# Sixteen tiles of expert-row sums: all on VectorE, or ten on VectorE and six on GpSimd

## What is computed

```
# layer 0: 16 experts, 2 for each token; layer 1: 32 experts, 8 for each token
for e in range(N_EXPERTS):
    h = silu(flat @ Wu[e]) * (flat @ Wg[e])
    out = out + combine[:, e:e + 1] * (h @ Wd[e])
...
routed = (down[unsort].reshape(T, K, H) * tkw[..., None]).sum(axis=1)
...
x = x + ffn(layernorm(x))
```

## Time and profile before

| | us |
|---|---|
| median of 3 runs | 1419.74 |
| lowest and highest | 1417.56 and 1423.05 |
| the profiled execution | 1433.71 |
| its span, first to last instruction | 1431.9 |
| layer 0, first load of yk to end of the last sum | 557.44 to 579.02 |
| layer 1, first load of yk to end of the last sum | 1371.67 to 1427.90 |

### The profile page before, as it was taken

How to read it: one execution, slowest core, us unless ns; L and a number is a source line. 1 busy time by engine, 2 the same in 40 slices (tenths; PEclk the granted TensorE clock), 3 DMA queues, 4 the chain that set the end, 5 groups by cost and what they waited for, 6 DMA issues and landing times. The chain is left out here.

```text
span 1431.9 us, 22633 instructions
## 1 busy us (share of the span) xinstructions
PE 1010.7 (71%) x6358; PEld 827.7 (58%) x6358; DVE 740.1 (52%) x1996; ACT 426.4 (30%) x1045; POOL 541.5 (38%) x740
## 2 busy tenths in 40 slices
PE   0289999998687894489998878660003999999910
PEld 0177777777554683377777756430003888887810
DVE  1677877774452355666555625620001555554567
ACT  1144444443110341134444322000001444444400
POOL 0022222221235363233333312366663566565610
PEclk9989999998679897599999975785556999999965
DMA  9000000000512453000000009133333556555467
GB/s 308 24 1 2 1 0 0 0 0 1 198 39 94 131 152 120 29 1 1 1 0 0 0 2 373 64 115 119 119 116 123 167 173 178 165 173 153 131 247 282
DMA packets 73707, 136.17 MB, mean 95 GB/s; under 512 B 14590, under 2 KB 52365, under 8 KB 71568
## 3 DMA queue, kind: packets, MB, share of 16 engines
q1 hardware_dynamic: 52016, 84.63, 18.5%
q0 software_dynamic: 17568, 46.71, 9.2%
q10 hardware_dynamic: 4032, 3.75, 0.8%
HBM read 78.66 MB, written 62.39 MB: 99 GB/s over the span
## 5 line engine op out<-in xcount | busy, mean ns | idle before, releaser
L1643 POOL DMA_INDIRECT parts<-e_y,e_dest x206 | 202.6, 984 | 176.4 <-issue 112.1
L996 POOL TENSOR_SCALAR_AFFINE_SELECT a_probs<-a_probs 128x256 f32<-128x256 f32 x256 | 110.0, 454 | 305.0 <-ACT a_probs L700 304.0
L1538 PE MATMUL e_ps_u<-wres,e_xT 128*128 x824 | 215.5, 385 | 0.1
L1251 POOL DMA_INDIRECT rows<-d_rows,d_place_at x160 | 153.6, 960 | 117.5 <-DMA rows<-d_rows,d_place_at 59.8
L1608 DVE TENSOR_TENSOR e_hid<-e_act_out,e_ps_u 128x128 f32<-128x128 f32 x206 | 59.3, 288 | 242.6 <-ACT e_act_out L1579 165.6
L1530 PE MATMUL e_ps_x<-ident,e_xg 128*128 128x128 f32 x412 | 80.4, 278 | 146.4 <-DMA e_xg<-rows 146.4
L1538 PEld LDWEIGHTS e_ps_u<-wres,e_xT 128*128 128x128 f32 x824 | 158.2, 193 | 23.1 <-issue 1.6
L1530 PEld LDWEIGHTS e_ps_x<-ident,e_xg 128*128 128x128 f32 x412 | 58.7, 144 | 169.0 <-DMA e_xg<-rows 148.1
L847 DVE TENSOR_REDUCE a_block_max<-a_ring 128x6 f32<-128x768 f32 x128 | 119.3, 950 | 22.2 <-PE a_ring L523 21.9
L1574 ACT ACTIVATE e_xT<-e_ps_x 128x256 f32<-128x256 f32 x206 | 78.9, 383 | 172.5 <-PE e_ps_x L1530 171.9
L700 ACT ACTIVATE a_probs<-a_ring 128x768 f32<-128x768 f32 x128 | 103.7, 810 | 82.0 <-PE a_ring L551 80.4
(11 more groups left out here) (220 smaller groups left out, 2124.3 us busy)
## 6 DMA issues: line engine op xcount, KB each, us to landing
e_xg<-rows SPq DMA_DIRECT2D x159, 160.0 KB
e_yk<-parts SPq DMA_DIRECT2D x16, 1024.0 KB, 6.6
wres<-in_experts SPq DMA_DIRECT2D x4, 3072.0 KB
e_xg<-rows SPq DMA_DIRECT2D x47, 144.0 KB
wres<-in_experts SPq DMA_DIRECT2D x4, 1536.0 KB
rows<-setup_empty SPq DMA_DIRECT2D x32, 160.0 KB
e_yk<-parts SPq DMA_DIRECT2D x16, 256.0 KB, 2.9
parts<-e_y,e_dest POOLq DMA_INDIRECT x206
```

The costliest lines, as they stand in the source:

```text
L996: last = nc.gpsimd.affine_select(out=diagonal[:, :, a], in_=diagonal[:, :, a], compare_op=ALU.is_ge, fill=0.0, base=0, pattern=[[0, 2], [1 ...
L1251: nc.gpsimd.indirect_dma_start(out=rows[:, :], out_offset=bass.IndirectOffsetOnAxis(ap=place_at[:, t, k:k + 1], axis=0), in_=X[:, t], in_o ...
L1538: last = nc.tensor.matmul(ps_u[b % 2][:, 0:2 * P], xT[b % 2][:, c * P:(c + 1) * P], wres[:, ds(e, 1), 2 * c * P:2 * (c + 1) * P].rearrange ...
L1643: nc.gpsimd.indirect_dma_start(out=parts[:, :], out_offset=bass.IndirectOffsetOnAxis(ap=dest[b % NY][:], axis=0), in_=y[b % NY][:], in_off ...
```

## The change

`POOL_TILES` names six of the sixteen tiles. These are summed by GpSimd, with the same adds as before, and the other ten by VectorE. Each engine has its own counter of finished tiles and its own counter for the waits between its adds. SP, before load t, waits on the counter of the engine that sums tile t-3; ScalarE, before a store, waits for each of its four tiles. Loads, buffers and stores are the same.

```diff
+POOL_TILES = (1, 3, 6, 8, 11, 13)
...
+        def tile_summed(eng, t):
+            done = summed_pool if t in POOL_TILES else summed_dve
+            eng.wait_ge(done, len([u for u in range(t + 1) if (u in POOL_TILES) == (t in POOL_TILES)]))
+
+        def add_parts(ops, t, eng, sums, done):
+            part = yk[t % NC]
+            eng.wait_ge(yk_loaded[t % NC], 16 * (t // NC + 1))
+            n = K * H // 2
+            while n >= H:
+                sums.inc(ops.tensor_tensor(part[:, 0:n], part[:, 0:n], part[:, n:2 * n], ALU.add))
+                sums.wait(eng)
+                n //= 2
+            ops.tensor_tensor(x[:, t], part[:, 0:H], x[:, t], ALU.add).then_inc(done, 1)
...
             for t in range(NT):
-                wait(sp, summed, t - NC + 1)
+                if t >= NC:
+                    tile_summed(sp, t - NC)
...
-                    act.wait_ge(summed, (q + 1) * NT // 4)
+                    for t in range(q * NT // 4, (q + 1) * NT // 4):
+                        tile_summed(act, t)
...
             for t in range(NT):
...
+                if t not in POOL_TILES:
+                    add_parts(nc.vector, t, dve, sums_dve, summed_dve)
...
+            sums_pool.start(0)
+            for t in range(NT):
+                if t in POOL_TILES:
+                    add_parts(nc.gpsimd, t, pool, sums_pool, summed_pool)
+            pool.wait_ge(summed_pool, len(POOL_TILES))
```

More of the change, by code:

```diff
@@ L1500, in expert_blocks @@
         yk_loaded = [sem(f"yk_loaded{i}") for i in range(NC)]
-        summed = sem("summed")
-        sums = Chain(sem("sums"), 1000)
+        summed_dve = sem("summed_dve")
+        summed_pool = sem("summed_pool")
+        sums_dve = Chain(sem("sums_dve"), 1000)
+        sums_pool = Chain(sem("sums_pool"), 1000)
         out_stored = sem("out_stored")
         block = ctx.enter_context(nc.Block())
+        def tile_summed(eng, t):
[10 more added lines that the diff above has]
+            ops.tensor_tensor(x[:, t], part[:, 0:H], x[:, t], ALU.add).then_inc(done, 1)
         def loaded(eng, b):
@@ L1626, in _ @@
                     weigh(i - 2, owner.pop(0))
-            sums.start(0)
+            sums_dve.start(0)
             for t in range(NT):
[L1629 to L1637, removed]
+                if t not in POOL_TILES:
+                    add_parts(nc.vector, t, dve, sums_dve, summed_dve)
+            dve.wait_ge(summed_dve, NT - len(POOL_TILES))
         @block.gpsimd
```

## The result

| | before | after |
|---|---|---|
| median of 6 runs, us | 1419.62 | 1431.63 |
| lowest and highest | 1417.56 to 1423.05 | 1429.00 to 1434.96 |
| ratio, 95% interval | | 1.0082 (1.0065 to 1.0099) |
| the profiled execution | 1433.71 | 1431.46 |
| layer 0, first load of yk to end of the last sum | 21.58 | 22.96 |

What follows compares the result with a forecast made beforehand. At the end no engine bounds alone: 48.8% of the chain is a load, 48.4% VectorE's adds. Layer 1 +7.7 and layer 0 +1.4 make +9.1 us; 1419.74 + 9.1 = 1428.9 us, range 1422.5 to 1435.

Steps and rivals of the forecast that it cites:

- GpSimd's tile: Layer 1: four GpSimd operations per tile take 5.12 us, 5.4 with gaps (4.2 to 5.6); VectorE's tile takes 2.76.
- rival 3: Sums of both layers: engines take turns, but GpSimd adds 512 columns in 1.04 us; +4.4 + 0.4, 1424.5 us; chance 0.10.
- Taking turns: Sums of both layers: adds with two SBUF operands on VectorE and GpSimd mostly run one after another; 0.13 us start-up overlaps.
- Rival 2: Sums of both layers: engines run side by side, not slower; +3.4 in layer 1, 1424.5 us in all; chance 0.13.
- Rival 1: Sums of both layers: whole instructions exclude each other, start-up included; +10.1 + 1.4 = +11.5, 1431.2 us; chance 0.17.
- Layer 1's sum: Layer 1, from the first add: 58.3 work - 3.6 overlapped start-ups + 4.7 idle = 59.3 us against 51.6, +7.7 us.
- The walk of the ring: Loads and sums followed tile by tile through three yk buffers; in layer 1, tile 15 ends 64.1 us after first issue.
- Layer 0's sum: Layer 0, by the same reckoning of loads and sums: 20.3 instead of 18.9 us, +1.4 us (+0.1 to +3).
- Costed at nothing: GpSimd's start after its scatters, the two counters, ScalarE's waits and the end after the last sum: no added time.
- What bounds the stretch: Layer 1: no engine alone, 48.8% a load, 48.4% VectorE's adds, transfers close behind; layer 0: loads and ring set the pace.
- rival 4: Layer 1: faster, loads flow at 2.77 us throughout, 53.1 against 56.2 us, at most -3; over 0.5% gain has chance 0.02.

Runs made afterwards that it cites:

- c_tt: Kernel before, plus 14 GpSimd adds of 128x1024 on spare buffers in layer 1 that nothing waits for; layer 1's stretch 82.6 us, 26.4 more.
- a_nc8: Changed kernel with eight yk buffers in place of three; ratio to the kernel before 0.9978 (0.9961 to 0.9996), layer 1's stretch 56.2 us.
- l1only: Changed kernel with only layer 1 shared, layer 0 summed by VectorE alone; ratio to the kernel before 1.0066 (1.0042 to 1.0091).
- l0only: Changed kernel with only layer 0 shared, layer 1 summed by VectorE alone; ratio to the kernel before 1.0033 (1.0002 to 1.0065).
- l0early: Changed kernel with only layer 0 shared and GpSimd on tiles 1, 2, 4, 5, 7, 8; layer 0's stretch 23.4 us, then 1.16 us wait.

## Why the prediction was nearly right, and where it was short

1. **GpSimd's tile.** Predicted 2.4 + 1.28 + 0.72 + 0.72 = 5.12 us; with VectorE idle it takes 2.34 + 1.26 + 0.72 + 0.72 = 5.04. The row with two operands of real columns, 1283 ns in the earlier trace rows, was the right one to scale (512 columns took 1.26 here), and 1043 ns, rival 3, would have been a fifth too low.
2. **Taking turns.** Read from attention's rows, where other instructions met, and shown for these by c_tt and a_nc8. Rival 2, side by side, is out: a VectorE add of 256 columns takes 2.44 us beside a GpSimd add of 1024, not 0.42. Rival 1, whole instructions that exclude each other, is out too: 0.28 us of each pair of instructions overlap, where I had taken 0.13 for each instruction, 0.26 a pair. Its total, 1431.2 us, is nearer to the measured 1431.63 than the forecast is, but that is chance: what the forecast lacked was not this overlap.
3. **Layer 1's sum.** The walk of the ring gave 59.3 us from the first add, and 59.0 were measured; tile 15 at 64.1 after the first issue, measured 63.9. The time in which neither engine added, short gaps between adds included, was 4.8 us, predicted 4.7. The term of +7.7 us came out as +7.67. That it fits to some hundredths is luck: in other profiled executions layer 1's shared stretch took 64.6 us (l1only) and the unshared one 56.0 and 56.4 (l0only, l0early), so the term is 7.7 within some half a microsecond. Single tiles were off by more: tile 2 was predicted at 17.2 and ended at 14.5, because VectorE kept pace with GpSimd instead of falling a tile behind.
4. **Layer 0's sum.** +1.4 predicted, +1.38 measured, and +1.05 in l0only.
5. **Costed at nothing.** This step failed. I had looked at when GpSimd begins its tiles, and not at what it must do after them to leave the block: a drain of 3.9 us, before the change hidden under 25 us of VectorE's sums, and now the last to arrive at the barrier. +1.58 us. The queue's row of the kernel before already had it, with 5.9 us, so it isn't so that GpSimd has nothing to do in that part. With these 1.58 the sum is 10.7, where the three stretches give 10.6 and the medians 12.0; the other 1.4 stay open.
6. **What bounds the stretch.** Right in that the ring's waits were a part. Wrong in how near I put the transfers' bound: I gave rival 4 at most 3 us, from 2.77 us for a load and 1.25 for a store. The 379 GB/s behind the 2.77 came from a stretch under the ring of three. Eight buffers saved 6.8 us in layer 1 on the same transfers, at 421 GB/s or 2.5 us a load; the pace of 3.0 us to which I had raised my walk was itself made by the ring. And in layer 0 I had named the loads beside the ring; there too the ring alone was at fault (21.6 to 15.9 us). The forecast of the change didn't depend on it, since both walks used the same pace.

## What to carry to other kernels

Before giving half of an elementwise loop to GpSimd, look for rows where its reads meet two-operand instructions of VectorE on SBUF; if those stretch, the two engines have one budget, and a tile on the slower engine costs its own slower time out of it. Look first at what the fast engine waits for: here one more buffer took 6.8 us off the stretch to which the second engine added 7.7. And when an engine gets work late in a block, its way out of the block becomes part of the critical path, drain included.

## What the runs showed of the hardware that I had not expected

- GpSimd's drain at the end of this block takes 3.9 to 4.1 us behind its adds and 5.8 to 6.0 us behind the scatters. It isn't the same everywhere: at the ends of the other blocks of the kernel before it takes 0.8 to 2.7 us. What sets its length was not tried.
- GpSimd's one-operand tensor_scalar of 1024 columns lasted 2.8 us when it began with VectorE idle and 3.4 us or more when it began under one of VectorE's 1024-column adds, longer than a two-operand add alone (2.3), yet held VectorE up by only 0.6 to 0.7 us.
- GpSimd's memsets of 1024 columns, 951 ns each, don't slow VectorE's two-operand adds at all.
- A reduction on VectorE of 2048 values that lie 1 KB apart takes 3.6 us, where the same sum by three halving adds takes 1.22 + 0.69 + 0.42 = 2.34.
- Where both engines have adds waiting, the turns alternate strictly, one instruction each, through all six pairs of a_nc8's layer 1.
